# Two transformer layers on one core: new job orders for the periods, whole 128-row tiles for the contexts, late loads and quantisation spread over periods

## The reference

```
x += self attention, 16 heads of 16, softmax   (a second layer norm with gamma, beta inside)
x += cross attention over the context, 16 heads of 16, softmax, with biases
x += linear 256 -> 256, weights rounded to int4, plus a rank-16 correction (a, b)
x += self attention, 16 heads of 16, sigmoid weights over their sum, RMS norm and rotation of q and k
x += cross attention over the context, one head of 256, softmax
x += hashed experts: the mean of each 128-row chunk, times 6 hyperplanes, picks two of 64
     expert matrices; the chunk's rows times both, times 0.5
```

## Time and profile before

| | |
|---|---|
| median of 3 runs | 1202.59 us |
| profiled execution: time, span | 1207.5 us, 1205.7 us |
| PE busy (TensorE matmul) | 1095.4 us, 91% |
| PEld busy (weight load) | 805.9 us, 67% |
| DVE busy (VectorE) | 792.3 us, 66% |
| ACT busy (ScalarE) | 639.7 us, 53% |
| POOL busy (GpSimd) | 601.1 us, 50% |
| mean granted TensorE clock | 0.96 |
| HBM read, written | 29.47 MB, 4.19 MB |

### The profile page before, as it was taken

The page is one execution under the profiler, slowest core; times in us unless marked ns, Lnnn a source line. Parts: engine busy times, 40 slices in busy tenths (PEclk is TensorE's granted clock), DMA queues, the critical chain, the costliest instruction groups (busy, mean ns, idle before and its releaser), DMA issues. The chain is left out here.

```text
span 1205.7 us, 24337 instructions
## 1 busy us (share of the span) xinstructions
PE 1095.4 (91%) x8458; PEld 805.9 (67%) x8458; DVE 792.3 (66%) x1748; ACT 639.7 (53%) x1192; POOL 601.1 (50%) x927
## 2 busy tenths in 40 slices
PE   6679999999989999999998899999999995999975
PEld 5346777777666777667666677767677664778753
DVE  5457777777766556666577878787778622476661
ACT  3135665656645765555554466666666672545430
POOL 4423444554463445554467877787878300024333
PEclk9679999999999999999999999999999997999995
DMA  8984566654852444433431767574758721035446
GB/s 212 152 95 54 80 82 103 82 66 78 106 58 56 73 81 85 79 82 79 79 68 22 86 74 85 66 89 59 93 67 96 92 25 36 13 93 176 129 140 192
DMA packets 123626, 104.94 MB, mean 87 GB/s; under 512 B 26841, under 2 KB 123241, under 8 KB 123497
## 3 DMA queue, kind: packets, MB, share of 16 engines
q1 hardware_dynamic: 118882, 100.76, 51.4%
q10 hardware_dynamic: 4624, 2.63, 1.0%
HBM read 29.47 MB, written 4.19 MB: 28 GB/s over the span
## 5 line engine op out<-in xcount | busy, mean ns | idle before, releaser
L616 ACT ACTIVATE l_probs<-l_sT 128x1024 f32<-128x1024 f32 (+1 forms) x320 | 325.4, 1022 | 91.4 <-PE l_o L972 50.5
L813 DVE TENSOR_REDUCE l_nmax<-l_ring 128x2 f32<-128x512 f32 (+1 forms) x384 | 255.1, 677 | 147.8 <-PE l_ring L987 146.0
L956 PE MATMUL l_sT<-qstack,kstack 99*128 99x256 bf16 (+2 forms) x1280 | 193.1, 274 | 9.5 <-DMA qstack<-l_qpart 5.0
L987 PE MATMUL l_ring<-kstack,qstack 96*128 96x256 bf16 (+1 forms) x1024 | 152.3, 253 | 24.9 <-DVE x_res L861 12.0
L972 PE MATMUL l_o<-l_probs,v_heads 128*32 128x256 f32 (+1 forms) x2560 | 161.2, 384 | 1.1 <-ACT l_probs L616 0.9
L956 PEld LDWEIGHTS l_sT<-qstack,kstack 99*128 99x128 bf16 (+2 forms) x1280 | 125.0, 105 | 35.9 <-ACT l_probs L616 6.0
L987 PEld LDWEIGHTS l_ring<-kstack,qstack 96*128 96x128 bf16 x1024 | 78.2, 99 | 86.3 <-issue 27.9
L1039 PE MATMUL l_ring<-wT,l_zT 128*128 128x256 f32 x512 | 124.4, 385 | 1.7 <-DVE l_nmax L813 1.5
L972 PEld LDWEIGHTS l_o<-l_probs,v_heads 128*32 128x32 f32 (+1 forms) x2560 | 72.1, 109 | 64.2 <-issue 19.0
L1019 PE MATMUL l_copy<-l_zT,wT 128*128 128x256 f32 x384 | 110.8, 417 | 4.3 <-ACT l_q L662 2.2
L1039 PEld LDWEIGHTS l_ring<-wT,l_zT 128*128 128x128 f32 x512 | 91.9, 190 | 20.8 <-issue 8.7
(11 more groups left out here) (193 smaller groups left out, 1928.0 us busy)
## 6 DMA issues: line engine op xcount, KB each, us to landing
qstack<-l_qpart SPq DMA_DIRECT2D x288, 128.0 KB, 4.1
kstack<-l_kpart SPq DMA_DIRECT2D x192, 128.0 KB, 5.8
t_experts<-in_experts SPq DMA_DIRECT2D x60, 256.0 KB, 3.0
kstack<-l_kpart SPq DMA_DIRECT2D x96, 60.0 KB, 3.1
out_y<-x_res SPq DMA_DIRECT2D x16, 256.0 KB, 3.7
x_res<-in_x SPq DMA_DIRECT2D x1, 2048.0 KB, 15.1
l_cx<-in_ctx SPq DMA_DIRECT2D x16, 90.0 KB, 2.9
t_cx<-in_ctx SPq DMA_DIRECT2D x16, 90.0 KB, 3.1
```

Source lines behind the costliest of these rows:

```text
L616: act.activation(probs[g % 4][0:kp, :], sT[g % 2][0:kp, :], ACT.Sigmoid if sig(u) else ACT.Exp, scale=HD ** -0.5).then_inc(p_ok, 1)
L813: dve.tensor_reduce(nmax[u % 2][:, tt, h0:h0 + hb], bank("s", u, i)[:, 0:hb * sk].rearrange("p (h k) -> p h k", h=hb), AX_X, ALU.max, nega ...
L956: i = pe.matmul(sT[g % 2][0:kp, j * S:(j + 1) * S], kstack[u % SLOTS][0:rows_used, col * width(u) + kt * kp:col * width(u) + (kt + 1) * kp ...
L987: m = pe.matmul(out[:, j * sk:(j + 1) * sk], qstack[u % SLOTS][0:STACK, (h0 + j) * S + tt * P:(h0 + j) * S + (tt + 1) * P], kstack[u % SLO ...
```

## The change

- The five hand-written orders, `ORDERS` of all three kinds, `FILL` and `FIRST_PERIOD`, are replaced.
- The transposed context has 128 rows in both halves: the second holds features 64 to 191, of which 64 to 127 stand in the first too. The weights of cross keys and values (`wT` 5 and 6, and `c_wk`, `c_wv` in the tail) carry zeros in rows 0 to 63 of their second half and the last 64 features below. All four or two matmuls of a projection then contract over 128 rows, and one ScalarE activation copies a transposed context where two did. The parts of the maxima are padded to 96 columns with zeros, and their transposition takes 96.
- The late loads are split: rows of ones in the filling (`l0`), weights in period 1 (`lo`), small tensors in periods 1 to 3 (`l1` in 2, `l2` in 3). Weight transpositions come one period later.
- `qq` becomes `q0` and `q1`: five steps over periods 12 to 14, each with its own semaphore step; `qA` moves from period 12 to 13, `qB` from 13 to 15.

```diff
     "self": """
-        np sT0 s qa s qb p0q dq0 s sT1 s pv2 e0 pv3 o1 e1 s
-        ka s kb p0k dk0 oT1 sT2 s e2 p1q dq1 p2q dq2 sT3 e3 nT p1k dk1 s p2k dk2 va rows vb s
-        pv0 pv1 o0 s aT s sT4 e4 s z cl s sT5 e5 oT0 xb s w ws qm qq qA
-        sT6 e6 pa st fac xs xf cx pb s sT7 e7 s lw lf qB""",
+        sT0 p0q qa s s qb np dq0 s sT1 s pv2 e0 pv3 o1 e1 s s ka s kb p0k dk0 p1q oT1 sT2 e2 dq1 p2q dq2 sT3 e3 nT p1k
+        dk1 s p2k dk2 lo l1 l2 va q0 rows vb s pv0 pv1 o0 s aT s s sT4 e4 s z cl e5 oT0 ws qm q1 s sT5 qA sT6 e6 fac xs
+        xb s w pa st cx xf pb sT7 e7 s lw lf qB""",
     "cross": """
-        np sT0 qa s qb p0q dq0 s sT1 pv2 e0 pv3 o1 e1 s
-        ka s kb p0k dk0 oT1 nT p1q dq1 p1k dk1 sT2 e2 s va fr vb p2q dq2 p2k dk2 rows rope_q rope_k
-        aT sT3 s fxb fz pv0 pv1 cx s o0 e3 xb cl
-        pa z st fst fac ffac pb qT fa fb oT0 kT s""",
+        np sT0 qa p0q qb s sT1 pv2 p0k e0 pv3 o1 s e1 s ka kb dq0 s dk0 oT1 p1q nT dq1 dk1 sT2 va fr vb p1k p2q rope_q
+        s rope_k aT e2 sT3 dq2 s rows s p2k fxb fz dk2 pv0 pv1 cx o0 e3 xb cl pa z fst fac ffac pb qT st fa fb oT0 kT s""",
     "sigmoid": """
-        sT0 qa qb rope_q sT1 p0q dq0 pv2 e0 pv3 o1 e1 ka kb rope_k
-        sT2 p1q dq1 p0k dk0 fr oT1 e2 sT3 va vb rows p1k dk1 p2q dq2 e3
-        pv0 pv1 o0 aT p2k dk2 sT4 fxb st fz e4 sT5 pa z pb e5 xb
-        sT6 fst fac ffac qT e6 fa fb sT7 oT0 kT e7""",
+        qa sT0 qb rope_q sT1 p0q dq0 pv2 e0 o1 e1 pv3 ka kb rope_k sT2 p1q oT1 e2 dq1 p0k dk0 va fr dq2 e3 vb rows dk1
+        p2q sT3 pv0 pv1 o0 aT p2k dk2 fxb sT4 st p1k fz e4 sT5 pa z pb e5 xb sT6 fac ffac fst qT e6 fa fb sT7 oT0 e7 kT""",
 }
 
 
 SPLIT = "p0q:{0} dq0:{0} ka:{0} kb:{0} p0k:{0} dk0:{0} {1} p1q:{0} dq1:{0} p1k:{0} dk1:{0} p2q:{0} dq2:{0} p2k:{0} dk2:{0}"
-FILL = ("xs:0 xf:0 wi rows:0 z:0 bi xs:1 xf:1 qa:0 qb:0 bv " + SPLIT.format(0, "rows:1 z:1") + " qa:1 qb:1 "
-        + SPLIT.format(1, "rows:2 z:2 xs:2") + " ll va:0 vb:0 s:0 s:0 qa:2 s:0 qb:2 "
-        + SPLIT.format(2, "s:0 s:0 rows:3 z:3 s:0 s:0") + " xf:2" + " s:0" * 9 + " np:0 s:1 s:1 nT:0")
+FILL = (
+    "xf:0 wi xs:0 rows:0 z:0 bi xs:1 xf:1 qa:0 qb:0 bv p0q:0 dq0:0 ka:0 kb:0 p0k:0 dk0:0 dk1:0 rows:1 z:1 p1q:0 "
+    "dq1:0 p1k:0 p2q:0 dq2:0 p2k:0 dk2:0 qa:1 qb:1 dq0:1 p0q:1 ka:1 kb:1 p0k:1 dk0:1 rows:2 z:2 xs:2 p1q:1 dq1:1 "
+    "p1k:1 dk1:1 p2q:1 dq2:1 p2k:1 dk2:1 l0 va:0 vb:0 s:0 s:0 qa:2 s:0 qb:2 p0q:2 dq0:2 ka:2 kb:2 p0k:2 dk0:2 s:0 "
+    "s:0 rows:3 z:3 s:0 s:0 p1q:2 dk1:2 dq2:2 dq1:2 p1k:2 s:0 s:0 s:0 s:0 s:0 s:0 s:0 s:0 s:0 np:0 s:1 p2q:2 s:1 "
+    "dk2:2 p2k:2 xf:2 nT:0")
 FIRST_PERIOD = (
-    "qa:3 s:1 s:1 qb:3 p0q:3 dq0:3 s:1 s:1 sT:0:0 s:1 sT:0:1 e:0:0 s:1 s:1 e:0:1 ka:3 s:1 kb:3 s:1 p0k:3 dk0:3 s:1 sT:0:2 s:1 "
-    "e:0:2 p1q:3 dq1:3 p2q:3 dq2:3 sT:0:3 e:0:3 s:1 s:1 p1k:3 dk1:3 s:1 p2k:3 dk2:3 np:1 s:2 va:1 rows:4 vb:1 nT:1 s:2 pv:0:0 "
-    "pv:0:1 o:0:0 s:2 s:2 sT:0:4 e:0:4 s:2 s:2 z:4 s:2 sT:0:5 e:0:5 s:2 oT:0:0 s:2 s:2 sT:0:6 e:0:6 s:2 s:2 s:2 "
-    "sT:0:7 e:0:7 s:2 s:2 s:2")
-
-W_AT = {1: 4, 2: 5, 3: 6, 4: 7, 6: 8, 7: 9, 8: 10, 9: 11}
-ONCE = {"lw": 5, "lf": 10, "qm": 11, "qq": 12, "qA": 12, "qB": 13}
+    "qa:3 s:1 s:1 qb:3 s:1 p0q:3 dq0:3 s:1 s:1 s:1 e:0:0 s:1 sT:0:0 sT:0:1 s:1 e:0:1 ka:3 kb:3 s:1 p0k:3 sT:0:2 "
+    "e:0:2 p1q:3 dq1:3 dk0:3 s:1 np:1 p2q:3 dq2:3 sT:0:3 e:0:3 s:1 s:1 s:1 p1k:3 dk1:3 dk2:3 s:1 p2k:3 s:2 va:1 "
+    "rows:4 vb:1 nT:1 s:2 pv:0:0 pv:0:1 s:2 s:2 z:4 o:0:0 s:2 e:0:4 sT:0:4 s:2 s:2 s:2 sT:0:5 e:0:5 s:2 oT:0:0 s:2 "
+    "s:2 sT:0:6 e:0:6 s:2 s:2 sT:0:7 e:0:7 s:2 s:2 s:2")
+
+W_AT = {2: 4, 3: 5, 4: 6, 5: 7, 7: 8, 8: 9, 9: 10, 10: 11}
+ONCE = {"lo": (1,), "l1": (2,), "l2": (3,), "lw": (5,), "lf": (10,), "qm": (11,), "q0": (12, 13, 14), "q1": (12, 13), "qA": (13,),
+        "qB": (15,)}
 X_AT = {p: p + 2 for p in range(1, 11)}
...
         if word in ONCE:
-            if p == ONCE[word]:
-                out.append((word, 0, 0))
+            if p in ONCE[word]:
+                out.append((word, 0, 2 * (p - 12) + (word == "q1") if word in ("q0", "q1") else 0))
             continue
...
-        nparts = sb("nparts", [P, TT, BF_PARTS, H], BF16)
+        nparts = sb("nparts", [P, TT, 2 * BF_PARTS, H], BF16)
...
-            def late_loads():
+            def ones_rows():
                 sp.wait_ge(ones_ok, 1)
                 for k in kstack[1:]:
                     sp.dma_start(k[STACK:STACK_M, :], kstack[0][STACK:STACK_M, :]).then_inc(ones_dma, 16)
...
+            def raw_weights():
                 for j in range(4, 8):
                     w_loads(sp, j, raw[j - 4], raw_dma[j - 4])
+
...
+            def bias_rows():
...
+            def tables():
...
-            def quantised():
-                pool.wait_ge(step_ok, 1)
-                link(pool.tensor_scalar(quant[:, :], ffn_w[:, :], inv_step, None, ALU.mult))
-                link(pool.tensor_scalar(quant[:, :], quant[:, :], 12582912.0, None, ALU.add))
-                link(pool.tensor_scalar(quant[:, :], quant[:, :], 12582912.0, None, ALU.subtract))
-                link(pool.tensor_scalar(quant[:, :], quant[:, :], -8.0, 7.0, ALU.max, ALU.min))
-                pool.tensor_scalar(quant[:, :], quant[:, :], step7, None, ALU.mult).then_inc(quant_ok, 1)
+            def quantised(step):
+
+                q = quant[:, :]
+                if step == 0:
+                    pool.wait_ge(step_ok, 1)
+                    i = pool.tensor_scalar(q, ffn_w[:, :], inv_step, None, ALU.mult)
+                else:
+                    pool.wait_ge(quant_ok, step)
+                    if step == 1:
+                        i = pool.tensor_scalar(q, q, 12582912.0, None, ALU.add)
+                    elif step == 2:
+                        i = pool.tensor_scalar(q, q, 12582912.0, None, ALU.subtract)
+                    elif step == 3:
+                        i = pool.tensor_scalar(q, q, -8.0, 7.0, ALU.max, ALU.min)
+                    else:
+                        i = pool.tensor_scalar(q, q, step7, None, ALU.mult)
+                i.then_inc(quant_ok, 1)
...
+            pool.memset(nparts[:, :, BF_PARTS:, :], 0.0).then_inc(pads_ok, 1)
+            for j in (5, 6):
+                pool.memset(t["wT"][0:2 * P - C, j, 1, :], 0.0).then_inc(pads_ok, 1)
...
-                act.activation(cxT[u % 3][:, 0, :], copy_bank[:, 0:SC], ACT.Identity)
-                act.activation(cxT[u % 3][0:C - P, 1, :], copy_bank[0:C - P, SC:2 * SC], ACT.Identity).then_inc(copy_empty, 1)
+                act.activation(cxT[u % 3][:, :, :].rearrange("p k s -> p (k s)"), copy_bank[:, 0:2 * SC],
+                               ACT.Identity).then_inc(copy_empty, 1)
...
-                        dve.wait_ge(quant_ok, 1)
+                        dve.wait_ge(quant_ok, 5)
...
-                pe.transpose(out[0:C - P, SC:2 * SC], cx[u % 2][:, P:C], ident[0:SC, 0:SC]).then_inc(copy_full, 1)
+                pe.transpose(out[:, SC:2 * SC], cx[u % 2][:, C - P:C], ident[0:SC, 0:SC]).then_inc(copy_full, 1)
...
-                    kp = (P, C - P)[k] if cross_k else P
-                    i = pe.matmul(copy_bank[:, mt * wd:(mt + 1) * wd], t["wT"][0:kp, W[kind_of(u)] + "qk".index(w), k, mt * P:(mt + 1) * P],
-                                  src[0:kp, k, 0:wd], start=(k == 0), stop=(k == KT - 1))
+                    i = pe.matmul(copy_bank[:, mt * wd:(mt + 1) * wd], t["wT"][:, W[kind_of(u)] + "qk".index(w), k, mt * P:(mt + 1) * P],
+                                  src[:, k, 0:wd], start=(k == 0), stop=(k == KT - 1))
...
-                    kp = (P, C - P)[k] if from_context else P
-                    i = pe.matmul(out[0:kq, tt * D:(tt + 1) * D], src[0:kp, k, tt * P:tt * P + kq],
-                                  t["wT"][0:kp, W[kind_of(u)] + "qkv".index(w), k, :], start=(k == 0), stop=(k == KT - 1))
+                    i = pe.matmul(out[0:kq, tt * D:(tt + 1) * D], src[:, k, tt * P:tt * P + kq],
+                                  t["wT"][:, W[kind_of(u)] + "qkv".index(w), k, :], start=(k == 0), stop=(k == KT - 1))
...
-                    i = pe.transpose(out[0:BF_PARTS * H, tt * P // 2:(tt + 1) * P // 2].bitcast(BF16),
+                    i = pe.transpose(out[0:2 * BF_PARTS * H, tt * P // 2:(tt + 1) * P // 2].bitcast(BF16),
...
-                sp.dma_start(w[name][0:rest, 1, :], d[name][P:P + rest, :]).then_inc(w_dma, 16)
+                sp.dma_start(w[name][P - rest:P, 1, :], d[name][P:P + rest, :]).then_inc(w_dma, 16)
...
+            for name in ("c_wk", "c_wv"):
+                pool.memset(w[name][0:2 * P - C, 1, :], 0.0).then_inc(pads_ok, 1)
...
-                act.activation(cxT[b % 2][:, 0, :], ctx_bank[:, 0:SC], ACT.Identity)
-                act.activation(cxT[b % 2][0:C - P, 1, :], ctx_bank[0:C - P, SC:2 * SC], ACT.Identity).then_inc(ctx_out, 1)
+                act.activation(cxT[b % 2][:, :, :].rearrange("p k s -> p (k s)"), ctx_bank[:, 0:2 * SC], ACT.Identity).then_inc(ctx_out, 1)
...
-                    for k, kp in ((0, P), (1, C - P)):
```

(7 more changed lines are left out.)

38 lines of the change are left out of this document (25 added, 13 removed).

## The result

The changed kernel takes 1143.06 us (median of 4 runs, 1137.4 to 1144.24) against 1203.12 us of the kernel before in the same session: a ratio of 0.948, 95% interval 0.945 to 0.952. That is 58 to 66 us faster; the medians are 60.1 us apart. The prediction was 1148 us, range 1138 to 1174. The profiled execution has a span of 1142.5 us against 1205.7, 63.2 less.

The account below looks back on a forecast made before the run. TensorE's own stream was taken as the bound, stack copies second, 0.4 us under it. Terms 36.5 + 7 + 6 + 7 + 2 + 4 + 1.5 = 64, less 9 struck (3 three times): 55; 1207.5 - 55 = 1152.5, less 4.9: 1148 us, range 1138 to 1174.

Parts of the forecast that it names:

- Whole tiles: 128-row matmuls in tail and cross units, 96-column maxima transposition: 15.5 + 14.5 + 6.5 = 36.5 us saved, bounds 28 and 40.
- Self order: Self periods: the 0.7 us wait for the residual addition goes; 0.7 for nine periods, 7 us, bounds 2 and 9.
- The slack of 0.4 us: Self periods: stack copies land about 0.4 us before the first maxima need them, a second bound under TensorE's.
- Cross order: Cross periods: waits go in 13 periods, 7 us less 1 for a new one; bounds 0 and 8.
- the waits of 0.57 a period: Cross periods: TensorE's waits for the residual addition and ScalarE's copy of the keys, expected to go.
- The 3 us struck where the two bounds meet: Cross periods: 3 us taken off the sum because TensorE's saving (1.6) and what the copies allow (1.7) are close.
- Sigmoid order: Sigmoid periods: VectorE normalises attention earlier, so a 0.7 us wait goes in ten periods; 7 us, bounds 0 and 10.
- Filling: Filling with first period: first stack 4 us later, but late DMAs moved out; 2 us gained, bounds 5 gained, 5 lost.
- Quantisation: Around period 13: the 4.16 us stall falls to 2 and part of the clock returns; 4 us, bounds 0 and 8.
- Transition: From cross to sigmoid periods: 1.5 us gained, bounds -3 and 4.
- the rival by which copies hold the layers: Late stacks leave only the slack; 25 self and cross periods lose 0.8 each, 20 us, 1168; chance 0.12.
- the rival by which whole tiles give nothing: A 128-row weight load waits for the matmul ahead of it; 36.5 us missing, 1185; chance 0.03.

Follow-up runs that it names:

- the orders alone: The changed kernel without the whole tiles (64-row second halves and 48 columns as before), new orders, spread loads and quantisation kept: ratio 0.968 to the kernel before, 38 us faster.
- the tiles alone: The kernel before with the whole 128-row tiles and 96 columns of maxima, orders, loads and quantisation as before: ratio 0.986 to the kernel before, 17 us faster.
- the statistics first: The changed kernel with one filling job moved, the first unit's statistics ahead of the first weights as before: 1140.02 us, ratio 0.947 to the kernel before.

## Why the prediction came out right, step by step

- **Whole tiles, 36.5 us taken, bounds 28 and 40: mis-sized.** The prices in the tail and the self units hold: keys 0.66 less (0.65 said), values 0.28 (0.27), the maxima 0.21 (0.20). In a cross unit it is 0.97 where 0.90 + 0.20 was charged: keys 0.66 and values 0.29, but the maxima give 0.12, and the context's transposition, charged at 0.05, takes 0.26 us before and after. (The products were rounded up as well: 0.90 x 16 and 0.2 x 32 make the sum 36.3.) And the change is only 21 us faster than the orders alone, 23 if the filling and the end, which scatter, are left out; the tiles alone bring 17. The failing step is "the steady tail is idle for only 2.3 us in 133, so I take it in full": the five tail periods with a choice did not get shorter (9.30 to 9.64 us before, 9.46 to 10.31 after), as VectorE's choice comes right behind the matmuls that got shorter, and the idle time of before said nothing about how far behind. The tail gave 8.2 us and its start 2.6, of 15.5. The maxima's 6.5 gave nothing in the self units, under the stack copies; 3 had been struck for that. The cross periods 16 to 25 gave 9.2, where ten times 1.1 was charged, and only with the new order.
- **Self order, 7 us: right.** 6.9 in eleven periods, from the orders alone. Of them 4.6 are idle time, the waits that the prediction counted, and 2.3 are less busy time, for which it had no term. The copies became the bound. The slack of 0.4 us that the prediction took from one unit was right for that unit (0.39), but before the change it went from 0.09 to 0.8 us over units 4 to 14, and at 0.09 a unit is already held by its copies.
- **Cross order, 6 us: right in size, partly by luck.** 5.6 in ten periods. But the prediction had the waits of 0.57 a period go, and the larger part of them, 0.35 for the residual addition, stayed. Idle time fell by 2.4 us in the ten periods, and 3.2 are less busy time, for which the sum had no term. The 3 us struck where the two bounds meet were not lost: the new order opened room for both.
- **Sigmoid order, 7 us: near**, and by its mechanism: 5.9 in ten periods, all of it idle time, and 2.5 in 42 to 47 that the sum left out.
- **Filling, 2 us: right in size by luck.** The 4 us later for the first rows were right (4.8), and so was it that the spread loads pay; their gain came through SyncE's queue, 17 us of issuing ahead of unit 2's copies. Of the 5.00 us wait at 70.27 nothing is left in the changed kernel, but the same old filling with the loads still in it had its last wait as 3.2 or 3.3 us in two other kernels, so part of it was one execution's. Against their start of period 1, 89.8 and 90.0 us, the new filling and first period gained nothing.
- **Quantisation, 4 us, bounds 0 and 8: mis-sized.** Periods 12 to 15 gave 6.4 by the orders alone, 1.7 of them idle time and 4.7 busy time. The cause was the one given: GpSimd's reduction. The stall is 2.5 us, now ahead of the maxima's transposition in period 12, and 0.7 in period 13. What was underpriced is the clock, which costs as much as the stall.
- **Transition, 1.5 us: mis-sized most.** Periods 26 to 31 gave 9.7 by the orders alone. They run in the cross order with the first sigmoid units' rotations in it. TensorE's idle time there fell from 11.7 to 4.0 us, so waits that the prediction did not read (577 to 693 us before, then 543 to 649 after) were most of it:

```profile
PE l_copy L1065 <- DVE l_attn L851: 3.4, 2, 2.0
PE l_copy L995 <- DVE l_z L801: 2.0, 3, 1.2
PE l_copy L995 <- ACT l_attnT L695: 1.7, 3, 0.6
```

```profile
PE l_copy L1023 <- DVE l_z L829: 1.1, 2, 0.6
```

The other 2.1 us are busy time: before, the granted clock was 0.89 from 657 to 673 us; with the new orders, tiles whole or not, it stays at 1.00 in this stage.

So the tiles were charged with 36.5 us, 27.5 if all that was struck is theirs, and gave 21; the rest of the sum was 27.5 and gave 42, of which 4.8 are the filling and period 0, most of that the scatter of one execution. The errors had opposite signs, and that the total came out within 5 us of the forecast is in good part luck.

Of the signs it named, these came: keys and values in the tail, self periods near 20.9 (20.97), cross near 14.0 (14.05), sigmoid near 20.1 (20.25), the wait ahead of the first scores. These did not: tail periods with a choice, the cross maxima's wait for the residual addition, the stall in period 13 (0.7 us, with 2.5 in period 12). And a sign of being wrong came in a mild form: TensorE's first maximum starts 0.09 us behind the last stack copy in nine of twelve self units, at a price of some 4 us, far below the 20 us of the rival by which copies hold the layers.

The keys are now eight matmuls of 128 rows in 0.88 us, where the 64-row halves made it 1.54: the rival by which whole tiles give nothing is out. The rule of the Trainium skill, "TensorE: Matmul & The Clock Gate", Part 3, that weight loads overlap running matmuls only when the row group differs, isn't seen in this kernel: in the tail stretch of 126 us weight loads are busy for 103.0 and matmuls for 118.2 us, so they overlap for at least 95.

None of the twelve other kernels is clearly faster than the changed one. The old filling with spread loads (0.947, 0.943 to 0.951) and the statistics first (0.947, 0.945 to 0.950) come nearest; their traces start period 1 by 5.3 and 4.2 us earlier, but their times are only 3.9 and 3.0 us under 1143.06, and the intervals overlap with that of the change. A largest weight found without GpSimd's reduction, which holds some 3 us, was not tried.

## What to carry to other kernels

A matmul that gets shorter pays only where nothing stands close behind it: before counting a saving in full, look up for each wait that is now zero how late its releaser is done, since an idle time of zero does not say whether the slack is 0.05 or 5 us. Here 0.90 us less of TensorE's work a period gave 0.35 in the old order and 0.92 in the new one, and nothing in tail periods with a long VectorE chain. Read the slack of several periods, not of one: it went from 0.09 to 0.8 us. Read every stretch of the profile, those between the steady states too: the transition held the largest gain, and no row of it had been read.

## What was unexpected of the hardware

- A reduction over partitions on GpSimd takes that engine for 13.6 us with 0.38 us shown as work, whether its input is ready 4.3 us before the instruction ahead of it ends or 2.6 us after; a copy in its place takes 0.19.
- With a stall of 4.2 us the granted clock was 0.88 on average in that period and 0.92 in the next (short drops from 2.4 to 1.2 GHz, one right behind the stall and one 20 us later); the same matmuls took 4.0 us longer. With the stall at 0.5 us the clock stayed at 1.00, and with the 2.5 us wait of the changed kernel too.
- Loads are dear in the queue that issues them: 20 of them, from one weight matrix to a column of biases, held SyncE's for 17 us, 0.4 to 3.3 us each.
- Among matmuls of 128 and 64 rows in turn (f32, 120 columns) the whole ones are as slow as the others: from the first of 64 rows on each starts 0.20 to 0.21 us after the last, and 0.11 where all have 128 rows.
